# Causal and window masks of a decoder's attention on one core: eight rank-one rows in the score stacks and four column-wise products per bank in place of one whole mask product

## What is computed

```python
# layer s
mask = (j <= i) & (j >= i - (W - 1))          # W = 64
scores = jnp.where(mask, scores, -jnp.inf)
# layer c
causal = jnp.tril(jnp.ones((S, S), jnp.bool_))
scores = jnp.where(causal[None, None], scores, jnp.float32(NEG))
```

## Time and profile before

| | us |
|---|---|
| median of 3 runs | 691.75 (690.23 to 692.27) |
| the profiled execution | 692.64 |
| its span, from the first to the last instruction | 690.6 |
| PE busy | 543.8 (79%) |
| PE weight loads busy | 421.6 (61%) |
| DVE busy | 339.0 (49%) |
| ACT busy | 218.3 (32%) |
| POOL busy | 147.5 (21%) |
| mean granted clock of TensorE | 0.909 |

### The profile page before, as it was taken

How to read it: one execution, slowest core, us unless ns; L and a number is a source line. 1 busy time by engine, 2 the same in 40 slices (tenths; PEclk the granted TensorE clock), 3 DMA queues, 4 the chain that set the end, 5 groups by cost and what they waited for, 6 DMA issues and landing times.

```text
span 690.6 us, 12843 instructions
## 1 busy us (share of the span) xinstructions
PE 543.8 (79%) x5092; PEld 421.6 (61%) x5092; DVE 339.0 (49%) x952; ACT 218.3 (32%) x491; POOL 147.5 (21%) x160
## 2 busy tenths in 40 slices
PE   5074939889898997997988668998687988998970
PEld 4052726656675765665666445777576866787860
DVE  3363615657577676776787547733333101232113
ACT  2000414354254453445445233453110100213103
POOL 4010003011021021031141650001111662322320
PEclk9577879999999999999999887999978989999995
DMA  4999654753935934935384462445555212688214
GB/s 109 202 181 131 211 85 65 96 59 63 121 45 84 113 44 74 113 47 79 48 108 72 84 160 60 152 170 178 203 180 181 62 36 58 191 251 282 32 13 131
DMA packets 56760, 78.97 MB, mean 114 GB/s; under 512 B 9294, under 2 KB 49357, under 8 KB 53628
## 3 DMA queue, kind: packets, MB, share of 16 engines
q1 hardware_dynamic: 42524, 39.64, 35.4%
q10 hardware_dynamic: 8032, 33.21, 15.3%
q0 software_dynamic: 6144, 5.29, 4.7%
HBM read 40.32 MB, written 13.74 MB: 78 GB/s over the span
## 4 chain that ended last, share of the span: by engine, by line
PE 33%; issue 8%; DVE 8%; DMA 3%; ACT 2%; SPq 1%; POOL 1%; ACTq 0%; another core or an unknown queue 0%; POOLq 0%; DVEq 0%
PE work L634 10%; PE work L648 8%; PE work L651 2%; PE work L442 2%; PE pv L560 2%; PE byk L496 1%; DVE negm L913 1%; PE work L436 1%; PE byk L492 1%; PE work L619 1%; DMA arena<-in_ffn_wi 1%; PE nat L496 1%; DVE r_c L984 1%; DVE stats_c L928 1%; PE work L599 1%
## 5 line engine op out<-in xcount | busy, mean ns | idle before, releaser
L913 DVE TENSOR_REDUCE negm<-nat 128x4 f32<-128x512 f32 (+2 forms) x192 | 120.5, 641 | 121.8 <-PE nat L496 116.6
L730 ACT ACTIVATE probs<-byk 128x512 f32<-128x512 f32 (+1 forms) x192 | 106.4, 563 | 131.1 <-PE byk L496 129.1
L496 PE MATMUL nat<-arena 96*128 96x128 bf16 (+2 forms) x512 | 74.9, 250 | 0.0
L496 PE MATMUL byk<-arena 99*128 99x128 bf16 (+2 forms) x512 | 73.1, 245 | 0.0
L1167 POOL TENSOR_TENSOR resk<-fk,parts_k 128x512 f32<-128x512 f32 x8 | 9.3, 1160 | 240.9 <-ACT fk L672 201.2
L492 PE MATMUL nat<-window_q,identb 128*128 128x384 bf16 (+1 forms) x96 | 36.5, 380 | 29.2 <-DMA arena<-parts_k 22.8
L496 PEld LDWEIGHTS nat<-arena 96*128 96x128 bf16 x512 | 47.6, 103 | 17.3 <-issue 3.9
L496 PEld LDWEIGHTS byk<-arena 99*128 99x128 bf16 x512 | 46.3, 100 | 18.6 <-issue 2.3
L492 PE MATMUL byk<-window_k,identb 128*128 128x384 bf16 (+1 forms) x96 | 34.5, 359 | 19.9 <-DMA arena<-mT 19.4
L634 PE MATMUL work<-woT,arena 128*128 128x160 f32 x256 | 46.5, 341 | 4.2 <-issue 4.0
L634 PE MATMUL work<-yn_T,arena 128*128 128x160 f32 x256 | 40.6, 313 | 10.6 <-DMA arena<-in_ffn_wi 6.0
(11 more groups left out here) (189 smaller groups left out, 951.5 us busy)
## 6 DMA issues: line engine op xcount, KB each, us to landing
arena<-parts_q SPq DMA_DIRECT2D x96, 128.0 KB, 5.0
arena<-parts_k SPq DMA_DIRECT2D x96, 128.0 KB, 5.3
arena<-in_ffn_wi ACTq DMA_DIRECT2D x12, 1024.0 KB, 4.9
arena<-in_ffn_wo ACTq DMA_DIRECT2D x12, 1024.0 KB, 8.2
expert_x<-fq ACTq DMA_DIRECT2D x1, 2600.0 KB, 12.6
v_s<-expert_x SPq DMA_DIRECT2D x20, 130.0 KB
xres<-in_x ACTq DMA_DIRECT2D x1, 2048.0 KB, 28.2
token_y<-xres SPq DMA_DIRECT2D x8, 256.0 KB, 2.2
```

What stands on the lines that cost most here:

```text
L496: last = nc.tensor.matmul(bank[:, i * w:(i + 1) * w], lhsT, rhs, start=False, stop=(i == heads - 1), skip_group_check=True)
L730: nc.scalar.activation(dst, src, ACT.Exp, scale=0.25).then_inc(exp_ready, 1)
L913: V.tensor_reduce(dst, src, AX, ALU.max, negate=True).then_inc(nat_free[job % 2], 1)
```

## The change

The mask is split in two. Whole 32x32 blocks of a sequence's 256x256 scores that are forbidden get their -3e38 from the score product itself: eight more rows (`NB`) in each stack, one for each block of 32 queries. In the q stack row a is 1 where the query lies in block a, otherwise 0; in the k stack row a is -3e38 where the key lies in a block forbidden to it, otherwise 0. The stacks so have `NR` = 104 rows, 107 with the three for the maxima. These rows are constants, made by POOL at the very start and sent by SP to each pair of stacks once (`block_rows`, two transfers of 64 and 88 KB). Where a pair of stacks passes from layer s to layer c (once for each of the four pairs), SP sends the k side's eight rows anew, from `past` (64 KB).

The blocks on the edges (the diagonal of both layers, and the block two before it in layer s) are still done by products with the identity, but these now go by 32 partitions of the bank: four products, each with 32 columns of the identity as stationary operand, writing to partitions 0, 32, 64 and 96 on, and only to the edge blocks of these rows.

```diff
-            def bank_scores(bank, mask, heads, w, at, emit_pair):
+            def bank_scores(bank, masks, heads, w, blocks_of, emit_pair):
 
-                mw = mask.shape[2]
-                nc.tensor.matmul(bank[:, 0:heads * w].rearrange("p (h t) -> p h t", t=w)[:, :, at:at + mw], identb[:, :],
-                                 mask[:, :, :].broadcast_to([P, heads, mw]), start=True, stop=False, skip_group_check=True)
+                by_block = bank[:, 0:heads * w].rearrange("p (h a c) -> p h a c", h=heads, c=BLK)
+                for r0, (first, kinds) in enumerate(blocks_of):
+                    n = kinds.stop - kinds.start
+                    rows_of = slice(r0 * BLK, (r0 + 1) * BLK)
+                    nc.tensor.matmul(by_block[rows_of, :, first:first + 2 * n - 1:2, :], identb[:, rows_of],
+                                     masks[:, kinds, rows_of].unsqueeze(1).broadcast_to([P, heads, n, BLK]),
+                                     start=True, stop=False, skip_group_check=True)
...
+            both, now, ahead = slice(0, 2), slice(1, 2), slice(0, 1)
+            n0_blocks = {"s": [(0, now), (1, now), (0, both), (1, both)], "c": [(r0, now) for r0 in range(4)]}
+            n1_blocks = {"s": [(r0, both) for r0 in range(4)], "c": [(4 + r0, now) for r0 in range(4)]}
+            t0_blocks = {"s": [(r0, both) for r0 in range(4)], "c": [(r0, ahead) for r0 in range(4)]}
+            t1_blocks = {"s": [(0, both), (1, both), (2, ahead), (3, ahead)], "c": [(r0, ahead) for r0 in range(4)]}
```

On SP (`block_rows(0)` stands ahead of everything but the first three loads):

```diff
+            def block_rows(pair):
+                for n, side in enumerate("qk"):
+                    last_row = NR if side == "q" else NR + MR
+                    sp.dma_start(stack[side, pair][KR:last_row, :, :], blocks[0:last_row - KR, n, :].unsqueeze(1).broadcast_to([last_row - KR, H, T]))\
+                        .then_inc(blocks_in[pair], 16)
+
+            sp.wait_ge(blocks_ready, 1)
+            block_rows(0)
...
                 if k >= PAIRS:
                     last_t(sp, k - PAIRS)
+                if side == "k" and k >= PAIRS and UNITS[k][0] != UNITS[k - PAIRS][0]:
+                    sp.dma_start(stack["k", k % PAIRS][KR:NR, :, :], past[:, :].unsqueeze(1).broadcast_to([NB, H, T]))\
+                        .then_inc(blocks_in[k % PAIRS], 16)
...
                 stack_side("k", k)
-                if k < PAIRS:
-                    if k == 0:
-                        sp.wait_ge(pool_cols, 1)
-                    sp.dma_start(stack["k", k][KR:KR + MR, :, :].rearrange("p h t -> p (h t)").rearrange("p (a b) -> p a b", b=P),
-                                 onesb[0:MR, :].unsqueeze(1).broadcast_to([MR, H * T // P, P])).then_inc(ones_in[k], 16)
+                if k + 1 < PAIRS:
+                    block_rows(k + 1)
```

PE's first N job of a unit waits in addition for `blocks_in` (units 0 to 3, and the four at which a pair of stacks changes its layer); the wait for `ones_in` before the T jobs goes. On POOL the six mask tiles become two (`mask_q`, `mask_k`, 128x256 each, four selects in place of ten), and before everything else come the constants of the rows:

```diff
+            g_.memset(blocks[:, :, :], 1.0)
+            link(g_.memset(past[:, :], 0.0))
+            link(g_.memset(blocks[0:NB, 1, :], 0.0))
+            keep(blocks[:, 0, :], 0, -BLK, 1, 0.0)
+            keep(past[:, :], BLK - 1, BLK, -1, NEG)
+            link(keep(blocks[0:NB, 1, :], BLK - 1, BLK, -1, NEG))
+            keep(blocks[:, 0, :], BLK - 1, BLK, -1, 0.0)
+            link(keep(blocks[0:NB, 1, :], 2 * BLK, -BLK, 1, NEG))
+            pool.sem_inc(blocks_ready, 1)
```

More of the change, by code:

```diff
@@ L25 @@
 MR = 3
+BLK = 32
+NB = T // BLK
+NR = KR + NB
 KEYS0 = {"s": 192, "c": 256}
@@ L172, in attention_and_experts @@
         identb = sb("identb", [P, P], BF16)
[L173 to L182, removed]
+        mask_q = sb("mask_q", [P, 2, P], BF16)
+        mask_k = sb("mask_k", [P, 2, P], BF16)
+        blocks = sb("blocks", [NB + MR, 2, T], BF16)
+        past = sb("past", [NB, T], BF16)
         ws = sb("ws", [P, C, 3 * D])
@@ L278, in attention_and_experts @@
         cleared = sem("cleared"); zeros_ready = sem("zeros_ready")
-        ident_ready = sem("ident_ready"); masks_ready = sem("masks_ready"); pool_consts = sem("pool_consts"); ones_in = sems("ones_in", PAIRS)
+        ident_ready = sem("ident_ready"); masks_ready = sem("masks_ready"); pool_consts = sem("pool_consts"); blocks_in = sems("blocks_in", PAIRS); blocks_ready = sem("blocks_ready")
         v_ones = sem("v_ones"); eps_ready = sem("eps_ready")
@@ L381, in MT @@
                 for i in range(MR):
-                    sp.dma_start(stack["q", k % PAIRS][KR + i:KR + i + 1, :, :], mT[i * H:(i + 1) * H, k % 2, :])\
+                    sp.dma_start(stack["q", k % PAIRS][NR + i:NR + i + 1, :, :], mT[i * H:(i + 1) * H, k % 2, :])\
                         .then_inc(m_rows[k % 2], 16)
@@ L505, in N @@
                     pe.wait_ge(stacked["k"][k % PAIRS], SIDE * (k // PAIRS + 1))
+                    if k < PAIRS:
+                        pe.wait_ge(blocks_in[k], 32)
+                    elif layer != UNITS[k - PAIRS][0]:
+                        pe.wait_ge(blocks_in[k % PAIRS], 48)
                 job = JOBS * k + j
@@ L511, in N @@
                     h0 = 4 * g
-                    last = bank_scores(bank, mq0[layer], 4, P, 0, lambda h: (q[0:KR, h0 + h, 0:P], ks[0:KR, h0 + h, 0:P]))
+                    last = bank_scores(bank, mask_q, 4, P, n0_blocks[layer], lambda h: (q[0:NR, h0 + h, 0:P], ks[0:NR, h0 + h, 0:P]))
                 else:
                     h0, w = 4 * g + 2 * (i - 1), KEYS0[layer]
-                    last = bank_scores(bank, mq1[layer], 2, w, w - mq1[layer].shape[2],
-                                       lambda h: (q[0:KR, h0 + h, P:T], ks[0:KR, h0 + h, T - w:T]))
+                    last = bank_scores(bank, mask_q, 2, w, n1_blocks[layer], lambda h: (q[0:NR, h0 + h, P:T], ks[0:NR, h0 + h, T - w:T]))
                 last.then_inc(nat_full[job % 2], 1)
@@ L532, in T_ @@
                     pe.wait_ge(m_rows[k % 2], 16 * MR * (k // 2 + 1))
-                    if k < PAIRS:
-                        pe.wait_ge(ones_in[k], 16)
                 job = JOBS * k + j
@@ L540, in T_ @@
                     h0, w = 4 * g + 2 * i, KEYS0[layer]
-                    last = bank_scores(bank, mk0[layer], 2, w, 0, lambda h: (ks[0:KR + MR, h0 + h, 0:P], q[0:KR + MR, h0 + h, 0:w]))
+                    last = bank_scores(bank, mask_k, 2, w, t0_blocks[layer], lambda h: (ks[0:NR + MR, h0 + h, 0:P], q[0:NR + MR, h0 + h, 0:w]))
                 else:
                     h0 = 4 * g
-                    last = bank_scores(bank, mk1[layer], 4, P, 0, lambda h: (ks[0:KR + MR, h0 + h, P:T], q[0:KR + MR, h0 + h, P:T]))
+                    last = bank_scores(bank, mask_k, 4, P, t1_blocks[layer], lambda h: (ks[0:NR + MR, h0 + h, P:T], q[0:NR + MR, h0 + h, P:T]))
                 last.then_inc(byk_full[job % 2], 1)
@@ L1112, in link, with keep @@
                 pool.wait_ge(pool_seq, seq[0])
-            def keep(m, base, cm, step):
-                return g_.affine_select(out=m[:, :, :], in_=m[:, :, :], compare_op=ALU.is_ge, fill=NEG, base=base,
-                                        pattern=[[0, 1], [step, m.shape[2]]], channel_multiplier=cm)
+            def keep(m, base, cm, step, fill):
+                return g_.affine_select(out=m, in_=m, compare_op=ALU.is_ge, fill=fill, base=base,
+                                        pattern=[[step, m.shape[1]]], channel_multiplier=cm)
+            g_.memset(blocks[:, :, :], 1.0)
[7 more added lines that the diff above has]
+            pool.sem_inc(blocks_ready, 1)
             g_.memset(ident[:, :], 0.0)
             g_.memset(identb[:, :], 0.0)
-            for m in (causal_q, window_q, window_q1, causal_k, window_k0, window_k1):
-                last = g_.memset(m[:, :, :], 0.0)
-            link(last)
+            g_.memset(mask_q[:, :, :], 0.0)
+            link(g_.memset(mask_k[:, :, :], 0.0))
             g_.affine_select(out=identb[:, :], in_=identb[:, :], compare_op=ALU.not_equal, fill=1.0, base=0,
@@ L1127, in _ @@
                              pattern=[[-1, P]], channel_multiplier=1).then_inc(ident_ready, 1)
[L1128 to L1137, removed]
+            keep(mask_q[:, 0, :], -1, -1, 1, NEG)
+            keep(mask_q[:, 1, :], 0, 1, -1, NEG)
+            keep(mask_k[:, 0, :], 0, -1, 1, NEG)
+            keep(mask_k[:, 1, :], -1, 1, -1, NEG).then_inc(masks_ready, 1)
             g_.memset(no_rows, NO_TOKEN).then_inc(zeros_ready, 1)
```

## The result

| | before | after |
|---|---|---|
| the profiled execution | 692.64 | 705.64 |
| its span | 690.6 | 703.3 |
| ratio after / before | | 1.0297 (95%: 1.0229 to 1.0365) |
| median on another chip, 5 runs against 23 of before | 686.8 | 703.7 |
| ratio there | | 1.0254 (1.0222 to 1.0287) |

The changed kernel is slower, by 3.0% on the first chip (about 20 us, 711 us in all) and by 2.5% or 17 us on the second. Medians are of all runs and ratios leave out disturbed ones, which is why the plain median of the four first runs is higher, 718.1 us (two of them took 720.3 and 1208.4). The forecast was 723.0 us in 703 to 747: right in sign and range, but its +31 us were half as much again as the +20 measured.

What follows compares the result with a forecast made beforehand. PE was taken to set the attention's pace. Span share 28, transfers 2, POOL 0.3 and clock 1 summed to +31.3 us: 692.64 became 723.9, with the median 0.9 lower, 723.0 us; range 703 to 747.

Steps and rivals of the forecast that it cites:

- its chain: Chain of waits from about 290 to 381.6 us: 0.48 of mask products on it by count, 0.60 by time.
- parts 1 to 3: PE's mask work: 41.0 us of columns saved, 80.9 us of visits at 0.24 us added, net +39.9 us.
- the merger with PV: Attention: 48 of 64 PVs directly ahead of a T job, whose masks share the column-wise visit, 9.1 us less.
- the signs: Expected in the profile after: mask group to first score 0.19 to 0.20 us at 128 columns, 0.17 at 64.
- part 4: Attention: 0.7 of PE's net added work lengthens the span, +28 us; ends 12 and 43.7.
- its lower end: Range's lower end: 0.48 x 24.5 = 12 us for the span, clock -3, together +9, about 701 us.
- parts 5 and 6: Start: larger transfers +2 us, POOL's new constants ahead of the identity +0.3 us.
- the path that I gave: Start: three larger pairs of transfers delay SP's rows of maxima and the first T job; POOL's identity 0 to 0.6 us late.
- part 7: PE's granted clock: emptier stretches against shorter waits, +1 us, ends -3 and +8.
- No cost of going in and out between bf16 products: Rival at the mask groups: a visit costs 0.03 us, span -18 us, 674 us; chance 0.08.
- The places in turn: Rival at the mask groups: the four places don't run together, +95 us on PE, 777 us; chance 0.04.
- The clock: Rival on PE: emptier streams bring clock 0.50 often, some 25 falls add 45 us, 768 us; chance 0.05.

Runs made afterwards that it cites:

- the rows alone: Kernel before with the eight rows, their transfers and POOL's constants, but the old whole mask product: 689.5 us, ratio 1.0066 to before.
- the waits filled: Kernel before without masks in the N jobs, plus 111 idle products in PE's waits: 675.7 us, ratio 0.9887; without idle products 682.1 us, 0.9958.
- no edge products: Changed kernel without any mask product, so its output isn't the reference's: 690.0 us, ratio 0.9976 to before.
- the visits alone: Kernel before with each whole mask product replaced by four column-wise ones over all old columns, no eight rows: 722.1 us, ratio 1.0517.
- the pairing: Changed kernel with both masks of two successive jobs done in one visit, then both jobs' scores: 691.2 us, ratio 1.0061 to before.

## Why the prediction was right, and where it was off

- *What bounds the kernel.* PE sets the pace of the attention when work is added: 35 us for 77, and 13 to 14 us for 36 (changed kernel against the rows alone, by ratio and by median). When work is taken away, much less comes back: 3 us for 31 (5 with the waits filled), 6 for 61 (no edge products against the rows alone). The prediction didn't need that second direction, and its chain, read for one kernel, doesn't show it.
- *Columns and visits (parts 1 to 3).* Saved columns as reckoned. A visit came to 0.23 us against my 0.24, the float32 PV was a fair stand-in, and the merger with PV is there (48 of 64 PVs in the trace). Of the signs, a group of 128 columns takes 0.17 us to the first score and one of 64 columns 0.14, where I wrote 0.19 to 0.20 and 0.17. Net on PE +36 us against +39.9.
- *How much reaches the span (part 4).* This is the term that was mis-sized. I took 0.7. The changed kernel gives 13 to 14 of 36, 0.36 to 0.39, the visits alone 35.3 / 77 = 0.46, the pairing 13 / 37 = 0.36. (What the clock took is in these shares.) My own first-order reading of the chain, 0.48 of the masks, was nearer than the value that I raised it to; the reason that I gave for raising it (more work puts PE on the chain more often) is not borne out, and PE's idle time took up more than I allowed for (27.3 to 18.0 us in the middle). With 0.39 x 39.9 = 16 us in place of 28 the sum would have been +19 and 711 us, which is what the ratio gives on the first chip. That is no second proof, since the 0.39 was measured on the same kernel. The range held because its lower end took 12 us for this term; the measured 13 to 14 lie close to that end.
- *Transfers and POOL at the start (parts 5 and 6).* I took +2.3 us; the rows alone cost 3 to 4.5. In the profile after, the path that I gave isn't there: SP sends the first rows of maxima at the same time as before, in spite of the larger pairs of transfers ahead of them (before, then after):

```profile
57.73 2.23 SPq L382 DMA_DIRECT2D arena<-mT  x3
57.68 3.15 SPq L390 DMA_DIRECT2D arena<-mT  x3
```

  POOL's identity came at 5.58 us, so PE was held by it, but it started at 5.71, no later than before:

```profile
5.29 0.29 POOL L1155 TENSOR_SCALAR_AFFINE_SELECT ident<-ident 128x128 f32<-128x128 f32 x1
5.71 9.18 PE L450 MATMUL work<-xT,ws 128*128 128x256 f32 x32 [5.71 <-POOL ident L1155]
```

  The first T job came at 67.5 us, not at 71, in that profile, and at 72.0 in the second one of the same kernel: the start varies by more than the term, and where the 3 to 4.5 us lie stays open.
- *The clock (part 7).* I took +1 us; the estimates above give 2 to 5. In the profile itself the middle has 0.95 against 0.98. The spread of the first chip's runs (705.6 and 715.9 us at 0.898 and 0.891) is larger than on the second and stays unexplained.
- *The rivals.* No cost of going in and out between bf16 products: wrong, the same 0.10 to 0.12 us each way is there between bf16 products, so it isn't float32's. The places in turn: wrong, 0.34 us for four times 512 columns. The clock: wrong as the main cause. PE's waits swallow most: right in that more than half of the added work was swallowed, and the measured +17 to +20 us lies midway between its +8 and my +31.

## What to carry to other kernels

Column-wise products run side by side, but each change from whole products to them and back costs PE 0.23 us here. They pay where one visit saves more than that in columns, some 550 at 2.4 GHz (an estimate from the two figures); this change saved 256 a visit. So gather them into few visits or put them next to others of the same form. Price a change on the busiest engine by the share of its work that the chain of waits shows, and don't assume that share for the opposite sign: this kernel's time grew by about 0.4 of the PE work that was added and fell by a tenth to a sixth of what was removed. Where a busy engine waits for some microseconds at known places, look at the clock behind the wait before reckoning a saving there.

## What the runs showed of the hardware

The four starts of a bf16 group of 64 to 512 columns lie so near to one another that its length is that of one product and about 0.12 us. The way in was about the same 0.10 us ahead of float32 and bf16 groups. No run separates what lies in the two ways, the array running empty or weights that nothing covers. Idle products inside PE's waits made four kernels, the one before among them, 0.4 to 0.7% faster by the ratios and raised their mean granted clock by 0.008 to 0.020: work that computes nothing was worth 2.5 to 4.9 us. One by one only the gain of before is clear of its interval, but all four point the same way.
